# Chunked gated attention on one core: blocks of 64 rows instead of 128, small products on quarters of the TensorE array

## The reference

```python
z = cumlogsumexp(s, axis=time); p = exp(s - z); g = exp(z_previous - z)
hk = hk * g[None, :] + k[:, None] * p[None, :]      # 64 x 64 state, row by row
ok = q @ hk;  pv = softmax(ok)                      # slot weights
hv = hv * g[:, None] + p[:, None] * v[None, :]      # 64 x 128 state
o  = pv @ hv
o  = o * rsqrt(mean(o*o) + eps) * g_norm_weight * silu(gate)
x  = layernorm(x + concat(o) @ Wo)
```

## Time and profile before

| | |
|---|---|
| median of three runs | 1897.66 us |
| profiled execution | 1898.23 us, its span 1896.5 us |
| PE busy | 98% of the span |
| DVE, ACT, POOL busy | 70%, 38%, 30% |
| granted TensorE clock, mean | 0.995 |

### The profile page before, as it was taken

One profiled execution on the slowest core, in us unless ns is written; L12 is line 12 of the kernel. 1 busy time (PEld: TensorE's weight loads), 2 busy tenths in 40 slices (PEclk: granted clock), 3 DMA queues, 4 the chain that ended last, 5 costly groups with the idle time before them and its releaser, 6 DMA issues.

```text
span 1896.5 us, 30417 instructions
## 1 busy us (share of the span) xinstructions
PE 1860.4 (98%) x11631; PEld 1369.8 (72%) x11631; DVE 1321.1 (70%) x2169; ACT 718.8 (38%) x1789; POOL 574.6 (30%) x595
## 2 busy tenths in 40 slices
PE   9999999999999999999999989999999999999998
PEld 7887888888878888888888764444434378888876
DVE  4666766666666666576666689999999765555556
ACT  3323222222222222223222227888888822222223
POOL 3041251332233133232322261444241322333232
PEclk9999999999999999999999998999999999999999
DMA  5213223231331322223122100111110211111112
GB/s 156 84 47 113 59 64 96 63 102 53 81 96 44 100 76 62 81 76 97 46 74 67 48 15 20 28 27 28 27 28 21 34 18 25 27 21 29 19 17 89
DMA packets 191232, 107.01 MB, mean 56 GB/s; under 512 B 112496, under 2 KB 174832, under 8 KB 191088
## 3 DMA queue, kind: packets, MB, share of 16 engines
q1 hardware_dynamic: 191088, 105.07, 21.1%
HBM read 62.74 MB, written 34.14 MB: 51 GB/s over the span
## 4 chain that ended last, share of the span: by engine, by line
PE 82%; DVE 9%; ACT 3%; POOL 2%; SPq 2%; DMA 1%; issue 1%; POOLq 0%; DVEq 0%; ACTq 0%
PE a_ps L59 18%; PE a_ps L61 17%; PE a_ps L60 17%; PE a_ps L1098 6%; PE a_ps L1060 5%; PE a_ps L1082 3%; PE a_ps L1263 2%; PE a_ps L1114 2%; PE a_ps L1042 2%; ACT x_prob L1716 2%; PE a_ps L1209 2%; DVE a_rz L1829 2%; PE a_ps L1246 1%; DVE a_raw_qks L1780 1%; PE a_ps L1186 1%; PE a_ps L1105 1%
## 5 line engine op out<-in xcount | busy, mean ns | idle before, releaser
L1780 DVE TENSOR_REDUCE a_raw_qks<-a_ps 128x1 f32<-128x512 f32 x512 | 321.1, 683 | 19.3 <-PE a_ps L1060 18.6
L1716 ACT ACTIVATE x_prob<-a_ps 128x512 f32<-128x512 f32 x512 | 279.9, 608 | 63.5 <-PE a_ps L1082 61.9
L59 PE MATMUL a_ps<-a_vg_hi,a_xT_lo 128*128 128x512 f32 x512 | 209.2, 409 | 0.0
L61 PE MATMUL a_ps<-a_vg_hi,a_xT_hi 128*128 128x512 f32 x512 | 200.6, 392 | 0.0
L60 PE MATMUL a_ps<-a_vg_lo,a_xT_hi 128*128 128x512 f32 x512 | 199.6, 390 | 0.0
L1822 DVE SCALAR_TENSOR_TENSOR a_gate<-a_gate,a_ps 128x256 f32<-128x256 f32 x128 | 53.9, 421 | 188.0 <-ACT a_gate L1597 188.0
L878 POOL TENSOR_TENSOR a_f<-a_rs 128x8 f32<-128x8 f32 x32 | 6.4, 201 | 510.6 <-ACT a_flat L1638 510.6
L59 PE MATMUL a_ps<-a_xT_hi,a_qks_lo 128*128 128x512 f32 x384 | 156.9, 409 | 0.4 <-DVE a_xT_lo L1811 0.4
L61 PE MATMUL a_ps<-a_xT_hi,a_qks_hi 128*128 128x512 f32 x384 | 150.3, 391 | 0.0
L60 PE MATMUL a_ps<-a_xT_lo,a_qks_hi 128*128 128x512 f32 x384 | 149.8, 390 | 0.0
L1060 PE MATMUL a_ps<-a_xT_lo,a_xT_hi 64*128 64x512 f32 x384 | 143.4, 461 | 2.6 <-DVE a_raw_qks L1780 1.8
(11 more groups left out here) (199 smaller groups left out, 4181.8 us busy)
## 6 DMA issues: line engine op xcount, KB each, us to landing
a_og_blocks<-a_og_turn SPq DMA_DIRECT2D x120, 128.0 KB, 2.5
a_og_turn<-a_og_blocks SPq DMA_DIRECT2D x30, 512.0 KB, 3.8
a_e_blocks<-a_e_turn SPq DMA_DIRECT2D x124, 64.0 KB, 1.8
a_e_turn<-a_e_blocks SPq DMA_DIRECT2D x31, 256.0 KB, 2.9
a_key_blocks<-a_keys_turn SPq DMA_DIRECT2D x124, 48.0 KB, 1.9
a_keys_turn<-a_key_blocks SPq DMA_DIRECT2D x31, 192.0 KB, 3.7
a_raw_vg<-in_L_attn_Wv_dram SPq DMA_DIRECT2D x8, 512.0 KB, 6.6
a_raw_vg<-in_L_attn_Wg_dram SPq DMA_DIRECT2D x8, 512.0 KB, 7.6
```

The source lines that it names most:

```text
L59: pe.matmul(out, w_lo, x_hi, start=start, stop=False)
L61: return pe.matmul(out, w_hi, x_hi, start=False, stop=stop)
L1716: nc.scalar.activation(prob[par][:, s % 4, :], score_bank(q, s, par), ACT.Exp, scale=X_SCALE).then_inc(exp_done[par], 1)
L1780: nc.vector.tensor_reduce(nm[:, q % 2, i % 4, par, i // 4:i // 4 + 1], max_bank(u, q, i, par), AX.X, ALU.max, negate=True).then_inc(max_re ...
```

## The change

Blocks have 64 rows (CHUNK), so there are 8 and 7 prefix states. Block c is row tile i = c // 2, half r = c % 2. Each small product is 64 x 64 weights on one quarter of the array: its rows and columns follow from which halves of the partitions its operands and its output lie in. In `values` the columns are `HALF[r ^ h]`: head 1's two halves of a row tile lie crosswise in its bank, and gating and square sums put them back. `keys_turn` now shares memory with `causal`. The part of the values that comes from states is a function of its own, issued right after the diagonals. For n <= 28 (LATE_OUT) the output projection goes behind Q, into the banks okb and tb, and all four adds go behind the reciprocals. The scan moves before `low_turned`. Wo's split moves from step j = 0 to j = 1.

```diff
+CHUNK = P // 2
+CHUNKS = T // CHUNK
+        state_banks = (tb, ob[0])
+        slot_banks = (okb, ob[1])
+        LATE_OUT = NSTEP - 4
+        def out_banks(n):
+            return (okb, tb) if n <= LATE_OUT else ob
...
-                if j == 0 and not at(p, 0):
-                    pool.wait_ge(wo_done, 4 * n)
+                if j == 1 and not at(p, 0):
+                    pool.wait_ge(wo_done, 4 * (n - 1))
                     split_wo(p)
...
 key_scores:
+                for c in range(CHUNKS):
+                    i, r = c // 2, c % 2
+                    rows = slice(c * CHUNK, (c + 1) * CHUNK)
                     for h in range(2):
-                        mm = pe.matmul(ch[h][:, rows], keys[HALF[h], rows], queries[HALF[h], rows], start=True, stop=True)
+                        mm = pe.matmul(ch[h][HALF[r], i * CHUNK:(i + 1) * CHUNK], keys[HALF[h], rows],
+                                       queries[HALF[h], rows], start=True, stop=True)
 key_states:
+                        mm = pe.matmul(ch[r][HALF[h], i * DK:(i + 1) * DK], key_rows[HALF[r], i, DK * h:DK * (h + 1)],
+                                       e[HALF[r], i, DK * h:DK * (h + 1)], start=True, stop=True)
 states:
+                        mm = pe.matmul(state_banks[r][HALF[h], i * DV:(i + 1) * DV], e[HALF[r], i, DK * h:DK * (h + 1)],
+                                       v[HALF[r], j % 2, i, h * DV:(h + 1) * DV], start=True, stop=True)
 slots:
+                wait(pe, added, 4 * (n - 1))
+                wait(pe, og_ready, 2 * n)
+                wait(pe, sq_done, 2 * n)
+                        mm = pe.matmul(slot_banks[r][HALF[h], i * CHUNK:(i + 1) * CHUNK], e[HALF[r], i, DK * h:DK * (h + 1)],
+                                       causal[HALF[r], h, i, :], start=(i == 0), stop=False, skip_group_check=True)
+            def slots_from_states(n):
+                for c in range(1, CHUNKS):
+                    pe.wait_ge(key_state_ready, (CHUNKS - 1) * n + c)
+                        mm = pe.matmul(slot_banks[r][HALF[h], i * CHUNK:(i + 1) * CHUNK], key_state[HALF[h], c - 1, :],
+                                       queries[HALF[h], c * CHUNK:(c + 1) * CHUNK], start=False, stop=True, ...)
+            def values_from_states(n):
+                for c in range(1, CHUNKS):
+                        pe.matmul(ob[h][HALF[r ^ h], i * P:(i + 1) * P], wT[HALF[h], c * CHUNK:(c + 1) * CHUNK],
+                                  state[HALF[h], c - 1, :], start=(c == 1 or c == 2), stop=False, ...)
 values:
+                        mm = pe.matmul(ob[h][HALF[r ^ h], i * P:(i + 1) * P], causal[HALF[r], h, i, :],
+                                       v[HALF[r], j % 2, i, h * DV:(h + 1) * DV], start=False, stop=True, ...)
...
 TensorE, step:
                 key_states(n)
+                slots(n)
                 states(n, j)
-                slots(n)
+                slots_from_states(n)
                 next_project(VG)
...
-                if not first:
+                if n > LATE_OUT:
                     project_out(n, pair0, (0, 1))
...
                 diagonals(n)
+                values_from_states(n)
                 next_project(Q)
+                if not first and n <= LATE_OUT:
+                    project_out(n, pair0, (0, 1, 2, 3))
+                pe.wait_ge(proj_done, PROJ * (n + 2))
                 values(n, j)
...
 ScalarE:
+            def place_sums(n):
+                act.wait_ge(sq_done, 2 * n + 1)
+                for r in range(2):
+                    sums = nc.scalar.copy(ss[HALF[r], :]...[:, :, 1], crossed_sums[HALF[1 - r], :])
+                sums.then_inc(sums_placed, 1)
 GpSimd, factor:
+                pool.wait_ge(sums_placed, n + 1)
...
 VectorE, step:
+                normalised_slots(n)
+                turn_keys(n + 1)
                 running_states(n)
-                turn_keys(n + 1)
-                normalised_slots(n)
...
                 slot_sum(n)
+                scaled_weights(n)
                 gating(n + 1, VG + 2, b1)
-                scaled_weights(n)
                 slot_reciprocals(n)
+                running_z(n + 1)
                 if not first:
                     low_turned(n)
+                if late:
+                    mask_diagonal_blocks(n)
                 gating(n + 1, VG + 3, b1)
...
                 inverse_z(n + 1)
-                gated_output(n, j, 1)
+                if not first and late:
+                    add_out(n, (j - 1) % B, (0, 1, 2, 3))
+                gated_output(n, j, 0)
```

More of the change, by code:

```diff
@@ L182, in layer_program @@
         rz = sb("rz", [P, T])
-        state = sb("state", [P, TT - 1, DV])
+        state = sb("state", [P, CHUNKS - 1, DV])
         v = sb("v", [P, 2, TT, 2 * DV])
         gate = sb("gate", [P, 2, TT, 2 * DV])
-        causal = sb("causal", [P, 2, T])
+        causal = sb("causal", [P, 2 * TT * CHUNK])
+        keys_turn = causal[:, :].rearrange("p (s i x) -> p s i x", s=4, x=32)
+        causal = causal[:, :].rearrange("p (h i c) -> p h i c", h=2, c=CHUNK)
         og = sb("og", [P, 2 * TT, DV])
@@ L839, in _ @@
                                     pattern=[[-1, P]], channel_multiplier=1).then_inc(const_ready, 1)
-            nc.gpsimd.affine_select(out=mask[:, 0, :], in_=mask[:, 0, :], compare_op=ALU.is_ge, fill=0.0,
+            nc.gpsimd.affine_select(out=flat[:, 0:P], in_=flat[:, 0:P], compare_op=ALU.is_ge, fill=0.0,
                                     base=0, pattern=[[1, P]], channel_multiplier=-1).then_inc(const_ready, 1)
@@ L1258, in values @@
                 pe.wait_ge(diag_masked, n + 1)
-                if n < NSTEP - 1:
-                    wait(pe, added, 4 * n)
-                for t in range(TT):
+                for c in range(CHUNKS):
+                    i, r = c // 2, c % 2
                     for h in range(2):
[L1263 to L1267, removed]
-                        mm = pe.matmul(ob[h][:, t * P:(t + 1) * P], wT[HALF[h], t * P:(t + 1) * P],
-                                       state[HALF[h], t - 1, :], start=False, stop=True, skip_group_check=True)
+                        mm = pe.matmul(ob[h][HALF[r ^ h], i * P:(i + 1) * P], causal[HALF[r], h, i, :],
+                                       v[HALF[r], j % 2, i, h * DV:(h + 1) * DV], start=False, stop=True,
+                                       skip_group_check=True)
                 mm.then_inc(o_done, 1)
@@ L1279, in transpose_keys @@
                 wait(pe, wT_ready, m)
-                transpose4(okb, [keys[:, i * P:(i + 1) * P] for i in range(TT - 1)]).then_inc(keysT_done, 1)
+                transpose4(okb, [keys[:, i * P:(i + 1) * P] for i in range(TT)]).then_inc(keysT_done, 1)
             def step(n, p, j, first):
@@ L1312, in step @@
                 pe.wait_ge(pv_ready, n + 1)
-                transpose4(okb, [pv[:, 2 * t:2 * t + 2, :].rearrange("p h m -> p (h m)") for t in range(TT)])\
+                pe.wait_ge(state_ready, (CHUNKS - 1) * (n + 1))
+                transpose4(tb, [pv[:, 2 * t:2 * t + 2, :].rearrange("p h m -> p (h m)") for t in range(TT)])\
                     .then_inc(pvT_done, 1)
@@ L1579, in copy_key_rows @@
                 act.wait_ge(keysT_done, m + 1)
-                nc.scalar.copy(key_rows[:, :, :].rearrange("p i c -> p (i c)"), okb[:, 0:(TT - 1) * P])\
+                nc.scalar.copy(key_rows[:, :, :].rearrange("p i c -> p (i c)"), okb)\
                     .then_inc(key_rows_ready, 1)
@@ L1859, in running_states @@
                 dve.wait_ge(states_done, n + 1)
-                nc.vector.tensor_copy(state[:, 0, :], tb[:, 0:DV]).then_inc(state_ready, 1)
-                for i in range(1, TT - 1):
-                    dve.wait_ge(state_ready, 3 * n + i)
-                    nc.vector.tensor_tensor(state[:, i, :], state[:, i - 1, :], tb[:, i * DV:(i + 1) * DV], ALU.add)\
-                        .then_inc(state_ready, 1)
+                nc.vector.tensor_copy(state[:, 0, :], state_banks[0][:, 0:DV]).then_inc(state_ready, 1)
+                for c in range(1, CHUNKS - 1):
+                    i, r = c // 2, c % 2
+                    dve.wait_ge(state_ready, (CHUNKS - 1) * n + c)
+                    nc.vector.tensor_tensor(state[:, c, :], state[:, c - 1, :], state_banks[r][:, i * DV:(i + 1) * DV],
+                                            ALU.add).then_inc(state_ready, 1)
             def low_oT(n):
@@ L1985, in step @@
                     reduce_max(0, 0, 0)
-                if not first:
+                if not first and not late:
                     add_out(n, (j - 1) % B, (0, 1))
@@ L1993, in step @@
                     reduce_max(0, 0, 2)
-                mask_diagonal_blocks(n)
+                if not late:
+                    mask_diagonal_blocks(n)
                 if norm_now and not into:
@@ L2048, in _ @@
                     low_x(1)
+            running_z(0)
             inverse_z(0)
             dve.wait_ge(const_ready, 2)
+            for r in range(2):
```

(2 more changed lines are left out.)

163 lines of the change are left out of this document (94 added, 69 removed).

## The result

The changed kernel takes 1847.24 us (median of 4, 1846.8 to 1848.68) against 1896.76 of the kernel before on the same chips: ratio 0.9739, 95% interval 0.9727 to 0.9751. That is 49.5 us less; 1858 was forecast, with a range of 1840 to 1883. One execution of the kernel of experiment 7 took 2267 us at a granted clock of 0.75, and no figure here includes it.

A forecast was written before the change was run, and what follows sets the result against it. TensorE, busy 98%, was taken to bound the kernel: 1897.7 - 49.6 (1.6 us a step over 31 steps) + 10.4 (stall at step 29) = 1858.5, stated as 1858 us, range 1840 to 1883.

The forecast's parts named there:

- TensorE is the bound: Whole span: PE busy 98%, so time taken from its queue comes off unless another engine becomes late.
- The price of a batch: Small fp32 products: passes on different array parts cost 0.110 us (128 columns) or 0.059 (64) together, however many parts.
- short-pass floor: Rival, chance 0.11: 64-column passes on quarters cost 25 ns each, using up the gain; 1898, no change.
- Both row halves into one bank: New values group: two row halves write one bank on different partitions, taken as free; otherwise saving 0.9 less a step.
- Saved per step: Eight small-product groups on TensorE: 1.4 to 1.75 us less a step, 1.6 taken, 50 us over 31 steps.
- entering and leaving: Time around small-product groups on TensorE beyond their batches: 0.75 us a step after, against 0.8 before.
- The prefix chain: VectorE's key state prefixes before slots from states: last ready after 1.95 us, PE there at 2.05, about nothing lost.
- The rival's late entry: Rival, chance 0.13: VectorE enters key prefixes 0.5 us later, PE waits 0.4 to 0.5 every step; +15, 1874.
- Step 29: SP waits for the moved Wo split; PE idles 8.4 us at the output projection, plus 2 for clock: 10.4.
- The last two steps: Different order at the end: saving and cost cancel within 2 us, the 1.6 of step 30 kept.
- likeliest case: Whole kernel, chance 0.64: saving 1.3 to 1.75 us a step, 5 to 16 lost at step 29; 1848 to 1873.
- The case on the other side: Rival, chance 0.07: only two array parts run at once; step +2.45 us, 1984, or 1945 at 33 ns.

The follow-up runs named there:

- experiment 7: The kernel before, with only the scan moved ahead of the second half of the turned output (right behind low_turned): 1889.5 us, ratio 0.9958.
- experiment 4: The changed kernel with every key score product issued twice into the same place: 1860.26 us, ratio 0.981.
- experiment 2: The changed kernel without crossing: head 1's values and gates lie as head 0's, so the values group has two quarters at a time: 1869.5 us, ratio 0.9856.
- experiment 3: The changed kernel with key scores, slots, diagonals and values issued for all even 64-row blocks before all odd ones: 1880.17 us, ratio 0.9911.
- experiment 9: The changed kernel with SP's row copies behind the keys, batch 0's normalisation moved to step 30, and slots laid crosswise: 1839.96 us, ratio 0.9707.
- experiment 1: The changed kernel with SP's wait for the last Wo split and the row copies moved behind get_keys: 1839.12 us, ratio 0.9693.
- experiments 6: The changed kernel with VectorE's scan (running sum) put back behind the key gates: 1854.7 us, ratio 0.9777.

## Why the prediction was right, and where it was off

- **TensorE is the bound.** Right: 98% busy before and after, 91% of the chain. What its queue lost came off the time.
- **The price of a batch.** Right. 110 ns for 128 columns and 59 for 64, for four quarters as for two: in the trace after, passes start 7 ns apart in fours, and the next four 58 ns (64 columns) or 109 ns (128) later. Sustained, scores cost 13.7 ns a pass in the steady step and diagonals 15.4. The trace after, and experiment 4 with 64 such passes in 1.04 us, 16 ns each, refute the short-pass floor; experiment 2 shows what two parts at once would cost, and with it that four do run. The Trainium skill, TensorE: Matmul & The Clock Gate, "Wait — 56ns, not 53.3ns?", has the floor of 25 ns; these runs do not agree.
- **Both row halves into one bank.** Right as taken, free: values 0.92 crossed, 1.80 straight (experiment 2). By the Trainium skill, TensorEngine Tiling (Array Packing), "Gotcha 1: PSUM Pressure", the crossed group would have to stay near 1.8. The measurement decides against it for rows that write different partitions.
- **Saved per step: 1.6, measured 1.85.** A term that was mis-sized. 1.76 of it are in the groups, which came to 5.79 where 7.55 - 1.6 = 5.95 was forecast; the rest, 0.09, lies between them. What was too large is the count of batches. The text gave 7 to 8 for 28 passes and took about the middle; with 7 everywhere and its 0.75 for entering and leaving, the sum is 5.06 + 0.75 = 5.81, against 5.79 measured. The starts show how this comes about: the next group starts while quarters are still busy with the last one (above, and experiment 3), so a last batch that isn't full is filled up by the next group. (The sum's upper end, 5.39, should be 5.34 by its own terms.)
- **The uneven steps: no term.** The text gave "most others 34.3" and did not ask why. They were 4.7 us, and the scan's move took them away (experiment 7). A term was missing, in the direction of faster.
- **The prefix chain: margin 0.1, "about nothing lost".** Right in the sum, and the times too: the last prefix was put 1.95 us behind the key states and came at 1.97, TensorE's last pair was put at 2.05 and came at 2.03. (By its own terms the chain is 0.2 + 0.25 + 6 x 0.24 = 1.89, so the margin stated was smaller than the terms give.) But the margin is gone, not kept: the last prefix sets the group's end (experiment 9). The rival's late entry did not happen; its condition, VectorE entering 0.5 later, was not met: VectorE idles 1.18 before that copy, 0.99 in the kernel before, so it was not late.
- **Step 29: 10.4 above a steady step, measured 42.44 - 31.96 = 10.5.** The wait is 7.0, 8.4 forecast, and the clock about 2.7, 2 forecast; the 0.8 left are in neither, since the step is still 2.2 above a steady one in experiment 1, with a wait of 1.4. Cause and place are right; that the sum fits to 0.1 is luck, errors of 1.4, 0.7 and 0.8 that cancel. SP's wait, the queue behind it and the clock are what experiment 1 takes away.
- **The last two steps: forecast to cancel, the 1.6 of step 30 kept.** Step 30 came out 3.5 shorter and the rest after it 1.6 longer, together -1.9.
- **Sum.** Forecast -49.6 + 10.4 = -39.2, measured -51.5 in the table. The 12.3 between them are 6.9 of the steady steps (27 x 0.255), 4.7 of the uneven ones, 0.2 in steps 0 and 1, 0.2 in step 29 and 0.3 at the end. All lie on the side of faster: the time is inside the stated range, but the 1.85 a step is above the likeliest case's 1.3 to 1.75, and 1847.24 just below its 1848 to 1873.
- **The case on the other side**, quarters that only pair off, had 0.07. Experiment 2 brings two parts at once about in one of the eight groups, the values, and it costs what was priced: 1.80, where the text said 1.75. So the price was right, and the mechanism is not there: with four different weights on four quarters, four passes start within some 20 ns in the trace after.

## What to carry to other kernels

When small products bound TensorE, count batches and not instructions: a quarter of the array costs as much as all four together, so give neighbouring products different rows and different columns of the array, even if one head has to be laid out crosswise for it. Then look for what comes too late once the groups are shorter: here nearly the whole gain hung on the later output projection. When a producer is moved by a step, look at each queue whose head waits for it; one such wait on SP cost 8 us. A steady step that is sometimes longer is a term of its own: look for the instruction whose duration is odd in that step.

## What was unexpected of the hardware

- Matrix passes do not all start in program order. With four quarters, passes for a free quarter start ahead of older ones for a busy quarter, across groups too, as in the rows of experiment 3 and in the changed kernel's own trace:
```profile
582.01 0.22 PE L1282 MATMUL a_ps<-a_queries,a_key_state 64*64 64x64 f32 x1
582.02 0.27 PE L1239 MATMUL a_ps<-a_v,a_e 64*64 64x128 f32 x1
```
  L1239 comes first in the program. The Trainium skill, TensorE: Matmul & The Clock Gate, "Part 3: Packing small matmuls — row/col tiling", says that matmuls start and end in program order; the starts in these two traces do not. Ends are modelled in the profile, and no run here shows them.
- VectorE's scan over 128x512 takes 1.2 us alone. Started while one of GpSimd's splits runs, it ends 1.08 us after that split (1.87, 2.7 or 3.8 long, experiments 6 and 7); started 0.40 us ahead of one, it takes 1.22.
- In TensorE's wait of 7.0 us the granted clock fell to the 1.2 GHz level, 2.7 us in, and it stayed there for 10.2 us; with a wait of 1.4 us in the same place it did not fall (experiment 1).
